# Layer 0's attention items: register-chosen rings of four buffers, mask arithmetic in the matmul, results transposed in one pass

## What is computed

```python
def _L0_xattn_ref(txt, image, kv_mask, q_mask, Wq, Wkv, Wout, bout):
    q = (txt @ Wq).reshape(b, n2, h, d).transpose(0, 2, 1, 3)
    kv = image @ Wkv
    k, v = jnp.split(kv, 2, axis=-1)
    ...
    dots = jnp.einsum('bhid,bhjd->bhij', q, k) * scale
    mask = q_mask[:, None, :, None] & kv_mask[:, None, None, :]
    dots = jnp.where(mask, dots, mask_value)
    attn = jax.nn.softmax(dots, axis=-1)
    out = jnp.einsum('bhij,bhjd->bhid', attn, v)
    ...
    return out @ Wout + bout
x = x + jnp.tanh(g_xattn[0]) * _L0_xattn_ref(_layernorm(x), ctx_1024, ...)
x = x + jnp.tanh(g_ffn[0]) * _L0_ffn_ref(_layernorm(x), ...)
x = x + jnp.tanh(g_xattn[1]) * _L1_xattn_ref(_layernorm(x), ctx_1024, ...)
x = x + jnp.tanh(g_ffn[1]) * _L1_ffn_ref(_layernorm(x), ...)
```

## Time and profile before

| what | value |
|---|---|
| median of three runs | 637.12 us (636.85 to 638.19) |
| the profiled execution | 635.04 us |
| its span, from the first instruction to the last | 633.3 us |
| mean granted TensorE clock | 0.901 |
| busy share: PE, DVE, ACT, POOL | 79%, 60%, 52%, 35% |
| the changed stage, within the span | about 88 to 165 us |

### The profile page before, as it was taken

The page is one execution under the profiler, slowest core; times in us unless marked ns, Lnnn a source line. Parts: engine busy times, 40 slices in busy tenths (PEclk is TensorE's granted clock), DMA queues, the critical chain, the costliest instruction groups (busy, mean ns, idle before and its releaser), DMA issues.

```text
span 633.3 us, 16642 instructions
## 1 busy us (share of the span) xinstructions
PE 498.6 (79%) x5784; PEld 373.9 (59%) x5784; DVE 383.0 (60%) x1148; ACT 328.1 (52%) x953; POOL 218.6 (35%) x406
## 2 busy tenths in 40 slices
PE   3885988777777997799999999999999857019930
PEld 2622225454753443688888888788888844009920
DVE  0579855565536544478777787787778744304512
ACT  2464844444221222587878787778787813005410
POOL 8293942223210000244444444344444410440035
PEclk9996978999786999799999999999999976559975
DMA  8994743443079984200000499900000069330122
GB/s 288 250 241 124 193 138 101 116 114 108 22 169 239 208 161 167 101 2 3 3 1 0 109 238 233 195 10 2 3 0 0 2 246 432 143 104 4 38 56 69
DMA packets 46843, 73.39 MB, mean 116 GB/s; under 512 B 4613, under 2 KB 40374, under 8 KB 45638
## 3 DMA queue, kind: packets, MB, share of 16 engines
q1 hardware_dynamic: 42588, 59.93, 37.4%
q0 software_dynamic: 1472, 8.72, 3.8%
q10 hardware_dynamic: 2730, 4.03, 2.1%
HBM read 69.06 MB, written 3.60 MB: 115 GB/s over the span
## 4 chain that ended last, share of the span: by engine, by line
PE 49%; DVE 20%; ACT 11%; issue 6%; DMA 6%; POOL 6%; ACTq 1%; POOLq 0%; DVEq 0%; SPq 0%
PE ps L1537 10%; ACT work L829 6%; PE ps L1551 6%; PE ps L1474 4%; PE ps L1663 3%; PE ps L1675 2%; PE ps L1508 2%; PE ps L1582 2%; DMA early_w<-in_ctx_blk 2%; POOL xe_scratch L716 2%; DMA region<-in_ctx_blk 2%; DVE sumsq L954 2%; DVE ps L1160 2%; POOL early_w L721 2%; PE ps L1354 2%
## 5 line engine op out<-in xcount | busy, mean ns | idle before, releaser
L829 ACT ACTIVATE work<-ps,nb,rkey 125x56 f32<-125x56 f32 x576 | 176.4, 404 | 52.2 <-DVE nb L1163 45.3
L1537 PE MATMUL ps<-work,region 128*64 128x96 f32 (+1 forms) x2304 | 116.9, 252 | 7.0 <-DVE work L1223 4.8
L1537 PEld LDWEIGHTS ps<-work,region 128*64 128x64 f32 (+1 forms) x2304 | 99.6, 137 | 18.9 <-issue 5.5
L1551 PE MATMUL ps<-region,work 125*64 125x129 f32 x1152 | 72.5, 273 | 4.5 <-POOL work L687 3.1
L687 POOL TENSOR_TENSOR work<-work,rs 125x336 f32<-125x336 f32 x96 | 71.9, 749 | 7.5
L1551 PEld LDWEIGHTS ps<-region,work 125*64 125x64 f32 x1152 | 64.1, 136 | 5.3 <-POOL work L687 3.6
L685 POOL TENSOR_TENSOR rs<-rs,rkey 125x6 f32<-125x6 f32 x96 | 19.2, 200 | 124.2 <-DVE rs L1175 124.2
L1160 DVE TENSOR_REDUCE ps<-ps 125x6 f32<-125x336 f32 x96 | 49.0, 510 | 18.6 <-PE ps L1537 18.1
L1171 DVE TENSOR_REDUCE sm<-work 125x6 f32<-125x336 f32 x96 | 47.4, 494 | 1.2 <-ACT work L829 0.6
L1382 PE MATMUL ps<-xln,folded 128*128 128x448 f32 x64 | 29.8, 591 | 10.3 <-ACT region L756 10.3
L954 DVE TENSOR_REDUCE sumsq<-region 125x12 f32<-125x1536 f32 (+1 forms) x16 | 27.7, 1746 | 7.9 <-ACT region L741 7.9
(11 more groups left out here) (294 smaller groups left out, 997.9 us busy)
## 6 DMA issues: line engine op xcount, KB each, us to landing
region<-in_w SPq DMA_DIRECT2D x6, 2048.0 KB, 18.1
region<-in_ctxT SPq DMA_DIRECT2D x16, 750.0 KB
early_w<-in_ctx SPq DMA_DIRECT2D x16, 672.0 KB
region<-in_ctx SPq DMA_DIRECT2D x16, 672.0 KB
work<-in_ctxT_blk SPq DMA_DIRECT2D x22, 187.5 KB
early_w<-in_w POOLq DMA_DIRECT2D x1, 4096.0 KB, 12.4
region<-in_ctx_blk ACTq DMA_DIRECT2D x11, 187.5 KB
early_w<-in_ctx_blk ACTq DMA_DIRECT2D x10, 187.5 KB
```

Of the source, the lines that this page charges most:

```text
L829: i = act.activation(shares_of(a, h)[:, c, :], ps[:CP, 2 + 2 * a + h, c * S:(c + 1) * S], ACT.Exp, bias=nb[:, a, q:q + 1], scale=rkey[:, b ...
L1537: mm = pe.matmul(ps[r0:r1, 2 + 2 * a + h, c * S:c * S + WIDE], keysT[:, s, c0 + r0:c0 + r1], qT[:, p, a * S:a * S + WIDE], start=True, sto ...
L1551: mm = pe.matmul(ps[i * COL:(i + 1) * COL, bank, 0:KW], A[:CP, i, h, c * S:c * S + COL], keys[:, 2 * p + i, h * CH + c, :], start=(h == 0 ...
```

## The change

Four buffers take the place of two for the transposed blocks (`ictxT`), the rows (`ictx`) and the mask rows. They lie in one tile each, and `item_buf` picks the buffer `(i % 2) * 2 + k` by a register. `ictx` and `ictxT` now lie in `msq2`, which the stage before uses for squares, so SP and ACT wait for its last sum (`key_ss`) before their first load. Loads are issued two items further ahead; each first waits for the landing of the load two items before it (`ld_itemT[k]`, `ld_item[k]`). In ACT's loop, `load_rows` moves from behind the copy of `PT` to ahead of it, at the loop's head.

POOL only converts the mask to `mask_b`'s first row, behind the copy of the queries; the second row holds ones. The mask matmul multiplies the two rows with constant rows of +1e30 and -1e30. `transpose_result` uses the transposing form, in one pass. Two fills for `mask_b` and two for `big_b` are added to POOL's constants.

```diff
+ITEM_BUFS = 4
...
-        mask_row = [carve(96, "work").bitcast(U8) for _ in range(2)]
+        mask_row = carve(ITEM_BUFS * 96, "work").bitcast(U8).rearrange("p (k m) -> p k m", k=ITEM_BUFS)
         mask_b = [carve(188, "work").bitcast(BF16) for _ in range(2)]
+        big_b = carve(64, "work").bitcast(BF16)
...
-        ictx = [carve(KC * 128, w).rearrange("p (c d) -> p c d", c=KC) for w in ("region", "early_rest")]
-        ictxT = [carve(KN, "work") for _ in range(2)]
+        ictx = msq2[:, 0:ITEM_BUFS * KC * 128].rearrange("p (k c d) -> p k c d", k=ITEM_BUFS, c=KC)
+        ictxT = msq2[:, ITEM_BUFS * KC * 128:ITEM_BUFS * (KC * 128 + KN)].rearrange("p (k m) -> p k m", k=ITEM_BUFS)
...
+        def item_buf(eng, i, k):
+
+            return bass.ds(eng.snap((i % 2) * 2 + k) if not isinstance(i, int) else i % 2 * 2 + k, 1)
...
-            def load_item(j, k):
+            def load_item(j, k, i):
+
                 blk = sp.value_load(item_blk[0:1, bass.ds(j, 1)], min_val=0, max_val=B * KB - 1)
-                sp.wait_ge(s_mm, j + 1)
...
+                to = item_buf(sp, i, k)
...
+            sp.wait_ge(key_ss, B + 2)
+            for k in range(2):
+                load_item(k, k, 0)
             with sp.Fori(0, (n + 1) // 2) as i:
                 for k in range(2):
...
+                    j = sp.snap(i * 2 + (k + 2))
+                    sp.wait_ge(s_mm, i * 2 + (k + 1))
+                    sp.wait_ge(ld_itemT[k], i * 32 + 32)
+                    load_item(j, k, sp.snap(i + 1))
...
+            for k in range(2):
+                gp.memset(mask_b[k][0:2, :], 1.0).then_inc(const, 1)
+            gp.memset(big_b[0:2, :], -BIG).then_inc(const, 1)
...
-            gp.wait_ge(const, CONSTS - 1)
+            gp.wait_ge(const, CONSTS - 2)
             gp.tensor_copy(before_b[:, :], before[:, :]).then_inc(const, 1)
+            gp.memset(big_b[0:1, :], BIG).then_inc(const, 1)
             gp.wait_ge(const, CONSTS)
...
-                gp.wait_ge(ld_itemT[k], loads)
                 gp.wait_ge(s_mm, j + 1)
                 gp.tensor_copy(Qk[k].rearrange("p (h q) -> p h q", h=H), tilesT[:, :, bass.ds(bt * QT, QT)])
-                gp.tensor_scalar(mask_b[k][0:1, 0:KN], mask_row[k][0:1, 0:KN], -1.0, BIG, ALU.add, ALU.mult).then_inc(q_tile, 1)
+                gp.wait_ge(ld_itemT[k], loads)
+                gp.tensor_copy(mask_b[k][0:1, 0:KN].unsqueeze(1), mask_row[0:1, item_buf(gp, i, k), 0:KN]).then_inc(q_tile, 1)
...
-            load_rows(0, 0)
+            act.wait_ge(key_ss, B + 2)
+            for k in range(2):
+                load_rows(k, k, 0)
...
                     j = act.snap(i * 2 + k)
+                    act.wait_ge(o_mm, j + 1)
+                    act.wait_ge(ld_item[k], i * 16 + 16)
+                    load_rows(j + 2, k, act.snap(i + 1))
                     act.wait_ge(pt_mm, j + 1)
                     act.wait_ge(o_mm, j + 2)
                     act.copy(PT[:KP].rearrange("p c r -> p (c r)"), ps[:KP, 2, 0:KC * 128]).then_inc(pt_ev, 1)
-                    load_rows(j + 1, 1 - k)
                     probabilities(j + AHEAD, k)
                     keep_result(j)
...
-                pe.matmul(ps[:, k, 0:KN], Qk[k], ictxT[k], start=True, stop=False)
-                pe.matmul(ps[:, k, 0:KN], ones_b[0:1, :], mask_b[k][0:1, 0:KN], start=False, stop=True).then_inc(s_mm, 1)
+                pe.matmul(ps[:, k, 0:KN], Qk[k], ictxT[:, item_buf(pe, i, k), :], start=True, stop=False)
+                pe.matmul(ps[:, k, 0:KN], big_b[0:2, :], mask_b[k][0:2, 0:KN], start=False, stop=True).then_inc(s_mm, 1)
...
-                pe.matmul(ps[:, 4, 0:128], On, ident[:, :], start=True, stop=True).then_inc(ot_mm, 1)
+                pe.transpose(ps[:, 4, 0:128], On, ident[:, :]).then_inc(ot_mm, 1)
```

More of the change, by code:

```diff
@@ L524, in _ @@
             n = sp.value_load(item_n[0:1, 0:1], min_val=1, max_val=ITEMS)
-            def load_item(j, k):
+            def load_item(j, k, i):
                 blk = sp.value_load(item_blk[0:1, bass.ds(j, 1)], min_val=0, max_val=B * KB - 1)
-                sp.wait_ge(s_mm, j + 1)
-                sp.dma_start(ictxT[k], t["ctxT_blk"][bass.ds(blk, 1), :, :].rearrange("a p c -> (a p) c")).then_inc(ld_itemT[k], 16)
-                sp.dma_start(mask_row[k][0:1, 0:KN], t["kv_blk"][bass.ds(blk, 1), :]).then_inc(ld_itemT[k], 16)
+                to = item_buf(sp, i, k)
+                sp.dma_start(ictxT[:, to, :], t["ctxT_blk"][bass.ds(blk, 1), :, :].rearrange("a p c -> p a c")).then_inc(ld_itemT[k], 16)
+                sp.dma_start(mask_row[0:1, to, 0:KN], t["kv_blk"][bass.ds(blk, 1), :].unsqueeze(0)).then_inc(ld_itemT[k], 16)
+            sp.wait_ge(key_ss, B + 2)
+            for k in range(2):
+                load_item(k, k, 0)
             with sp.Fori(0, (n + 1) // 2) as i:
                 for k in range(2):
[L534 to L537, removed]
+                    j = sp.snap(i * 2 + (k + 2))
[3 more added lines that the diff above has]
+            for k in range(2):
+                sp.wait_ge(ld_item[k], (n + 1) // 2 * 16 + 16)
             sp.wait_ge(x_new, 2)
@@ L630, in _, with item_queries @@
             n = gp.value_load(item_n[0:1, 0:1], min_val=1, max_val=ITEMS)
-            def item_queries(j, k, loads):
+            def item_queries(j, k, i, loads):
                 bt = gp.value_load(item_bt[0:1, bass.ds(j, 1)], min_val=0, max_val=BT)
-                gp.wait_ge(ld_itemT[k], loads)
                 gp.wait_ge(s_mm, j + 1)
                 gp.tensor_copy(Qk[k].rearrange("p (h q) -> p h q", h=H), tilesT[:, :, bass.ds(bt * QT, QT)])
-                gp.tensor_scalar(mask_b[k][0:1, 0:KN], mask_row[k][0:1, 0:KN], -1.0, BIG, ALU.add, ALU.mult).then_inc(q_tile, 1)
+                gp.wait_ge(ld_itemT[k], loads)
+                gp.tensor_copy(mask_b[k][0:1, 0:KN].unsqueeze(1), mask_row[0:1, item_buf(gp, i, k), 0:KN]).then_inc(q_tile, 1)
             for k in range(AHEAD):
-                item_queries(k, k, 32)
+                item_queries(k, k, 0, 32)
             with gp.Fori(0, (n + 1) // 2) as i:
                 for k in range(2):
-                    item_queries(gp.snap(i * 2 + (k + AHEAD)), k, i * 32 + 64)
+                    item_queries(gp.snap(i * 2 + (k + AHEAD)), k, gp.snap(i + 1), i * 32 + 64)
             gp.tensor_copy(ident_b, ident[:, :]).then_inc(pair_ok, 1)
@@ L780, in keep_result, with load_rows @@
                 act.copy(tilesT[:, :, bass.ds(dst * QT, QT)], ps[:, 4, 0:128].rearrange("p (h q) -> p h q", h=H)).then_inc(ot_ev, 1)
-            def load_rows(j, k):
+            def load_rows(j, k, i):
                 blk = act.value_load(item_blk[0:1, bass.ds(j, 1)], min_val=0, max_val=B * KB - 1)
-                act.dma_start(ictx[k][:KP, :, :], t["ctx_blk"][bass.ds(blk, 1), :, :].rearrange("a (p c) d -> (a p) c d", c=KC)).then_inc(ld_item[k], 16)
+                act.dma_start(ictx[:KP, item_buf(act, i, k), :, :], t["ctx_blk"][bass.ds(blk, 1), :, :].rearrange("a (p c) d -> p a c d", c=KC)).then_inc(ld_item[k], 16)
             act.wait_ge(items_ok, 1)
             n = act.value_load(item_n[0:1, 0:1], min_val=1, max_val=ITEMS)
-            load_rows(0, 0)
+            act.wait_ge(key_ss, B + 2)
+            for k in range(2):
+                load_rows(k, k, 0)
             for k in range(AHEAD):
@@ L1405, in _, with item_scores @@
             mm.then_inc(keep_mm, 1)
-            def item_scores(j, k, loads):
+            def item_scores(j, k, i, loads):
                 pe.wait_ge(ld_itemT[k], loads)
                 pe.wait_ge(q_tile, j + 1)
-                pe.matmul(ps[:, k, 0:KN], Qk[k], ictxT[k], start=True, stop=False)
-                pe.matmul(ps[:, k, 0:KN], ones_b[0:1, :], mask_b[k][0:1, 0:KN], start=False, stop=True).then_inc(s_mm, 1)
+                pe.matmul(ps[:, k, 0:KN], Qk[k], ictxT[:, item_buf(pe, i, k), :], start=True, stop=False)
+                pe.matmul(ps[:, k, 0:KN], big_b[0:2, :], mask_b[k][0:2, 0:KN], start=False, stop=True).then_inc(s_mm, 1)
             def transpose_result(j):
@@ L1421, in _ @@
             for k in range(AHEAD):
-                item_scores(k, k, 32)
+                item_scores(k, k, 0, 32)
             with pe.Fori(0, (n + 1) // 2) as i:
@@ L1430, in _ @@
                     mm.then_inc(pt_mm, 1)
-                    item_scores(j + AHEAD, k, i * 32 + 64)
+                    item_scores(j + AHEAD, k, pe.snap(i + 1), i * 32 + 64)
                     transpose_result(j)
@@ L1435, in _ @@
                     for c in range(KC):
-                        mm = pe.matmul(ps[:, 3, 0:128], PT[:KP, c, :], ictx[k][:KP, c, :], start=(c == 0), stop=(c == KC - 1))
+                        mm = pe.matmul(ps[:, 3, 0:128], PT[:KP, c, :], ictx[:KP, item_buf(pe, i, k), c, :], start=(c == 0), stop=(c == KC - 1))
                     mm.then_inc(o_mm, 1)
@@ L1706 @@
 SMALL = 20
-CONSTS = 29
+CONSTS = 33
 PLAN_LISTS = 38
```

## The result

The changed kernel takes **653.37 us** (median of 4 runs, 651.51 to 657.67) where the kernel before takes 636.99 (4 runs, 636.32 to 638.19): a ratio of 1.0265, 95% interval 1.021 to 1.032. The forecast was 640.7 us, in a range of 634.9 to 646.0: the direction was right, the size was not. Medians here are of all executions; ratios and their intervals leave out the few in the chip's slower state.

The account below looks back on a forecast made before the run. The prediction saw a row transfer ending last in the items stage, with ACT setting the pace after the change. Terms +2.2, -0.2, +1.0 and +0.6 made +3.6 us on 637.12: 640.7 us, range 634.9 to 646.0.

Parts of the forecast that it names:

- The order: Items stage: ACT's row load stands between result copy and L819 copy, uncovered by a wait; row transfer leaves the chain.
- The loop's length: Items stage: ACT's two-item loop becomes 7.15 us, 3.58 an item against 3.46, over 19 intervals +2.2 us.
- The rival of the clock: Items loop: a longer gap at the start or sparser loop costs PE its upper clock, 663 us; chance 0.05.
- The table read: In ACT's load block: 0.28 us by the profile; with the skill's 0.6 floor, loop 7.47 us and term +5.2.
- New constants: POOL's constants at the start: four added fills delay PE's first matmul and everything after, +1.0 us.
- First loads: Start of items stage: item 0's loads wait for the last sum of squares and land later, +0.6 us.
- SP and POOL: Items stage: SP's loads run up to four items ahead and POOL has waiting to spare, so both cost 0.
- the mask row's split DMA: SP's mask load in the items stage: shape changes from 1x375 to 15x25, covered like SP's other loads, 0.
- the last result's one-pass transpose: Behind the items loop: one pass in place of two passes of 128 columns, -0.2 us.
- the masks' plain copy: POOL, each item: a plain copy replaces add and multiply, 0, even if the copy is no shorter.
- the one-pass transpose of the other results: Inside PE's items loop: no effect on time, because PE has slack once ACT sets the pace.

Follow-up runs that it names:

- pe_numbers: The changed kernel with PE's loop written out for four items, so PE's buffers have fixed numbers: 654.96 us, ratio 1.0277.
- filled: The changed kernel with three extra products in every second item, where PE waits for ACT's copy of the transposed probabilities: 648.18 us, ratio 1.0111.
- before_ahead: The kernel before, two buffers, with only the row load moved ahead of the copy of the transposed probabilities: 643.18 us, ratio 1.0105.
- all3: sp_numbers with ACT's result copy ahead of the next exponentials and POOL's weight loads behind the first two items' queries and masks: 631.81 us, ratio 0.9875.
- rows_behind: The changed kernel with ACT's row load put back behind the copy of the transposed probabilities: 633.81 us, ratio 0.9957.
- sp_numbers: rows_behind with SP's loop written out for four items, fixed buffer numbers and the mask row as one transfer: 632.67 us, ratio 0.9948.
- changed_again: The changed kernel itself, run again as the base of a later set: 654.31 us, ratio 1.0255.

## Why the prediction was wrong, point by point

**The order: right.** The block stands between L797 and L819, the row transfer is out of the chain, ACT's wait for the maximum shrank, POOL's for transfers nearly vanished. Putting the block back takes away the whole loss (-19.6 us), clock included, and brings the rings' gain: pairs of 6.1 us.

**The loop's length: the step that failed**, "3.58 us an item against 3.46 ... +2.2 us". It has two errors. The first is of size: at full clock two items take 7.48 us, where the working had 7.15. The hand-over from ACT's copy to PE's product was put at 0.08 us, an estimate from other sequencer rows, and is 0.30 in that chain, because PE's register operations for the ring's address come behind the wait (0.13 in pe_numbers, without them); DVE adds 0.1. The rest of the working holds: from the result copy to L819 it has 1.97 us, and 1.99 were measured in filled. By 7.48 the term would have been 19 x (3.74 - 3.49) = +4.8, the forecast 643.3, still inside the range. Against before_ahead's 6.98 this loop pays 0.50 us a pair for the ring: some 0.2 in that hand-over, some 0.2 from the result copy to the next copy on ACT (1.99 against 1.75), the rest in DVE's wait.

The second is the clock. "At 3.46 us an item the clock was full, so at 3.58 I expect it too" reasoned from the pace. PE now waits up to 2.2 us in one piece for ACT's copy, in every second item, its clock falls to the lower level (1.2 of 2.4 GHz) and comes back, over and over, and what PE does at the lower level takes longer. Four products in that wait gave 10.2 us back. The rival of the clock had 0.05, and its price, 22 us more, was for a clock lost throughout; it came true in part. In the profiled executions the two make the loop's 15.7 us: some 4.7 by its length at full clock (19 x 3.74 = 71.1 us against 66.4), and some 11 by the clock (82.1).

**The table read: right.** It takes 0.30 us in the block (0.28 before). The Trainium skill, "DMA: Bandwidth & Descriptors", Latency and other measured facts, has a floor of 0.6; no read in the traces here is that long (0.29 and 0.46 in all3, at most 0.56 in any). That the 7.47 us worked out from it is what the loop took is chance.

**New constants: right in place, without effect that shows.** PE's first matmul starts at 10.04 us, not 9.02: +1.02. But the first query copy came at 84.56 instead of 86.98, and between 84.5 and 88 us in the other changed kernels. The stage before varies by more than this term, and no run shows why; its granted clock doesn't say (0.88 from 10 to 84 us in the changed kernel, which came early, 0.93 before). The term's undoing was not tried.

**First loads: mis-sized.** The mask copy waited 3.7 us for a landing at 88.6, and the first scores could start only then:

```profile
89.22 1.59 PE ps L1432 x2
```

SP issued that mask row at 82.61, as the stage before ended 2.0 us earlier here than in the kernel before (its last sum of squares at 81.3 instead of 83.3). The row took 6.0 us to land, where the working had 2.4 from its start of 85.1 (the lone row), 4.2 (with the weights) and at worst some 5.7 (all queued up). Counted from the end of that sum, the first scores start 7.9 us later, against 4.7 before (88.00): 3.2 us in place of +0.6, and 7.9 to 8.0 in rows_behind, sp_numbers and changed_again as well. That this shows so little in the total is luck, by the early end of the stage before.

**SP and POOL: right to cost nothing there,** but the mask row's split DMA, "covered in the same way", was covered only by ACT's long loop. Without that, in rows_behind, POOL waits 33.9 us for the mask rows again (98 to 160 us), and SP's issuing comes near the bound.

**Left open:** the last result's one-pass transpose (-0.2) and the masks' plain copy were not tried by themselves; both are below the scatter. Untried, too, is the one-pass transpose of the other results, which the prediction put at nothing because PE has slack: with more slack the clock fell, and this part's share in that stays open.

## What to carry to other kernels

A load that a computing engine issues is part of that engine's instruction stream: before moving it, find the wait that hides it now, and see whether one hides it at the new place. The Trainium skill, "DMA: Bandwidth & Descriptors", Issuing engines are not separate DMA queues, says that issuing is usually small beside the transfer. Here, with its table read and address, it was 1.5 us beside a transfer of 4.6, and its place decided the sign: behind the copy, 0.9957 of the time before, ahead of it, 1.0265. When a change leaves PE a longer wait in one piece, or less to do, price the loop at either clock, and don't take the clock from the pace.

## What was not expected of the hardware

PE got faster by being given useless work: with three or four products in its wait, pairs of 8.2 to 9.1 us went to 7.48 to 7.51 wherever the clock stayed up. And the same mask row of 375 bytes costs SP 0.27 to 0.30 us to issue to an address fixed in the code, and 0.94 to 1.06 when the buffer comes from a register, where it goes out as 15 pieces of 25 bytes.
